# Routed experts on the tokens that chose them: a fused transformer block, before and after

## The reference, cut to what matters

```python
x = x + tanh(g_xattn[0]) * attention(layernorm(x), cache=ctx)           # stage A
x = x + tanh(g_ffn[0])   * ternary_ffn(layernorm(x))                    # hidden width 682
x = x + tanh(g_xattn[1]) * wkv(w, u, layernorm(x), ctx)                 # recurrence over 64 tokens
x = x + tanh(g_ffn[1])   * experts(layernorm(x))

def wkv_step(p, q, o, k, v):              # per channel, o is a running maximum
    no = maximum(o, u + k); A = exp(o - no); E = exp(u + k - no)
    y = (A * p + E * v) / (A * q + E)
    no2 = maximum(w + o, k); A2 = exp(w + o - no2); E2 = exp(k - no2)
    return (A2 * p + E2 * v, A2 * q + E2, no2), y

def experts(x):                           # 8 experts, F = 128, 2 of them for each token
    shared = silu(x @ shared_gate) * (x @ shared_up) @ shared_down      # FS = 256
    probs = softmax(x @ router_w); vals, ids = top_k(probs, 2)
    combine = zeros(N, 8).at[arange(N)[:, None], ids].add(vals)
    y = einsum("enf,efd->end", silu(x @ w_gate[e]) * (x @ w_up[e]), w_down)
    return shared + einsum("ne,end->nd", combine, y)
```

## Time and profile before

| what | value |
|---|---|
| median of 3 runs | 811.62 us (809.74 to 812.77) |
| span of the profiled execution, first to last instruction | 806.8 us |
| TensorE busy | 741.4 us, 92% |
| PE weight loads | 642.7 us, 80% |
| VectorE busy | 633.1 us, 78% |
| GpSimd busy | 398.0 us, 49% |
| ScalarE busy | 384.9 us, 48% |
| mean granted TensorE clock | 0.975 |

### The profile page before, as it was taken

The page is one execution under the profiler, slowest core; times in us unless marked ns, Lnnn a source line. Parts: engine busy times, 40 slices in busy tenths (PEclk is TensorE's granted clock), DMA queues, the critical chain, the costliest instruction groups (busy, mean ns, idle before and its releaser), DMA issues.

```text
span 806.8 us, 13118 instructions
## 1 busy us (share of the span) xinstructions
PE 741.4 (92%) x4582; PEld 642.7 (80%) x4582; DVE 633.1 (78%) x1043; ACT 384.9 (48%) x730; POOL 398.0 (49%) x382
## 2 busy tenths in 40 slices
PE   6988799889999999989998999989998999968896
PEld 5876687778888788878887888878887988746785
DVE  2857589687978798888989798888979797899532
ACT  3536434556355644654455645653465635431321
POOL 1024332364746365464636465455546464565364
PEclk8999979999999999999999999999999999988999
DMA  8170002010022013110032113110121000101121
GB/s 249 53 208 1 1 1 53 27 54 27 27 79 67 27 38 81 45 47 13 26 78 66 35 30 78 55 37 26 43 74 53 26 26 26 41 26 40 34 73 51
DMA packets 35895, 41.19 MB, mean 51 GB/s; under 512 B 3118, under 2 KB 27096, under 8 KB 35864
## 3 DMA queue, kind: packets, MB, share of 16 engines
q1 hardware_dynamic: 35864, 40.78, 17.6%
HBM read 36.45 MB, written 4.33 MB: 51 GB/s over the span
## 4 chain that ended last, share of the span: by engine, by line
PE 59%; DVE 15%; issue 4%; POOL 3%; ACT 1%; DMA 1%; DVEq 0%; POOLq 0%; ACTq 0%
PE sums L475 14%; PE gate_ps L475 13%; PE up_ps L475 12%; PE transit L475 6%; DVE wk L1389 3%; DVE wk L1394 3%; PE transit L540 3%; PE transit L467 3%; PE transit L552 3%; DVE wk L1396 2%; POOL act_sb L1139 2%; PE transit L520 1%; POOL hid_l L1130 1%; DVE act_sb L1379 1%; DVE za_l L1333 1%
## 5 line engine op out<-in xcount | busy, mean ns | idle before, releaser
L1130 POOL TENSOR_TENSOR hid_l<-act_sb,hid_h 128x512 fp32r<-128x512 f32 (+1 forms) x128 | 173.3, 1354 | 171.9 <-ACT hid_h L917 171.9
L917 ACT ACTIVATE hid_h<-act_sb 128x512 fp32r<-128x512 f32 (+1 forms) x128 | 80.4, 628 | 150.9 <-POOL act_sb L1139 117.8
L1139 POOL TENSOR_TENSOR act_sb<-act_sb,late 128x512 f32<-128x512 f32 x64 | 92.0, 1438 | 100.2 <-DVE act_sb L1381 80.9
L1379 DVE SCALAR_TENSOR_TENSOR act_sb<-act_sb,gate_ps 128x512 f32<-128x512 f32 (+1 forms) x128 | 85.8, 670 | 68.9 <-ACT act_sb L901 68.9
L475 PE MATMUL sums<-down_h,hid_h 128*128 128x256 f32 x320 | 92.3, 288 | 12.7 <-POOL hid_l L1130 12.7
L475 PE MATMUL sums<-down_h,hid_l 128*128 128x256 f32 x320 | 90.0, 281 | 0.0
L475 PE MATMUL sums<-down_l,hid_h 128*128 128x256 f32 x320 | 90.0, 281 | 0.0
L1381 DVE TENSOR_TENSOR act_sb<-act_sb,up_ps 128x512 f32<-128x512 f32 x120 | 82.4, 687 | 4.1
L901 ACT ACTIVATE act_sb<-gate_ps 128x512 f32<-128x512 f32 x80 | 47.2, 590 | 71.4 <-PE up_ps L475 66.1
L475 PEld LDWEIGHTS sums<-down_h,hid_h 128*128 128x128 f32 x320 | 60.9, 190 | 19.8 <-issue 17.9
L475 PE MATMUL gate_ps<-zm_h,gate_h 128*128 128x512 f32 x140 | 62.3, 445 | 5.6 <-DVE act_sb L1381 5.6
(11 more groups left out here) (194 smaller groups left out, 1962.7 us busy)
## 6 DMA issues: line engine op xcount, KB each, us to landing
late<-combine_rows SPq DMA_DIRECT2D x64, 256.0 KB, 3.2
ctx_tok<-in_ctx SPq DMA_DIRECT2D x8, 512.0 KB, 4.9
vals<-in_ctx SPq DMA_DIRECT2D x16, 256.0 KB, 5.6
out_x<-late SPq DMA_DIRECT2D x8, 512.0 KB, 3.2
xa<-in_x SPq DMA_DIRECT2D x7, 512.0 KB, 3.5
wk<-in_L_ffn_w SPq DMA_DIRECT2D x2, 682.0 KB
late<-in_L_ffn_w_down SPq DMA_DIRECT2D x1, 1024.0 KB, 6.6
wk<-in_L_ffn_w_gate SPq DMA_DIRECT2D x2, 512.0 KB, 4.4
```

What stands on the lines that cost most here:

```text
L917: nc.scalar.activation(hid_h[0:n, pos], act_sb[0:n, pos], ACT.Copy).then_inc(hid_h_set, 1)
L1130: nc.gpsimd.tensor_tensor(hid_l[0:n, pos], act_sb[0:n, pos], hid_h[0:n, pos].bitcast(F32), ALU.subtract).then_inc(hid_l_set, 1)
L1139: nc.gpsimd.tensor_tensor(act_sb[:, pos], act_sb[:, pos], comb_sb[:, pos], ALU.mult).then_inc(weighted, 1)
L1379: nc.vector.scalar_tensor_tensor(mine, mine, 1.0, gate_ps[pos][0:hidden_rows(chunk)], ALU.add, ALU.mult).then_inc(gated_one, 1)
```

## The change

It does six things.

- Stages get lags of their own: P (first normalisation of a block, z0), A (attention), F (its feed-forward), N (normalising F's result for the recurrence), W, M. All twelve turns, -1 to 10, are written out, with one order of the pieces on each engine; pieces of stages that are off in a turn fall away.
- M keeps the two shared chunks in the turn. The eight expert chunks leave it, and with them the combine weights' way through DRAM.
- In M's place in the turn, tokens get places in lists: the router gives each token a first and a second choice (rank 0 and 1); TensorE counts by matmuls with ones (`place`), VectorE makes place numbers (`dispatch`), and GpSimd scatters each token's row by indirect DMA into a list in DRAM, by expert and rank: 8 scatters for each block.
- After the loop SP ends the 16 lists with padding rows (`end_lists`), VectorE makes tables of which tile of 128 rows belongs to which expert, and 76 tiles (38 for each rank) run in 19 groups of four. SP reads a tile's row number into a register and loads the tile; TensorE transposes it, reads the expert's number into a register (twice for each tile) and runs 6 + 3 matmuls of 256 columns with that expert's weights; ScalarE, VectorE and GpSimd work on the group. Rank 0 results are scattered to rows in DRAM; for rank 1 GpSimd fetches those by indirect DMA, VectorE adds, and GpSimd scatters the sums to the output.
- F's chunks are pipelined one deep: up(c + 1), then down(c). On ScalarE tanh(c + 1) stands ahead of the high part of c.
- The recurrence goes without a running maximum: keys' exponentials come with the decay folded in by two more rows in the product z2_T, four scans run on them, and add_now is two fused operations.
- A turn's idle matmuls fall away but in the first turns.

The diff, cut; a line of "..." stands for what is left out. In order: the lists on top, SP, TensorE, ScalarE, GpSimd, VectorE.

```diff
-TRANSIT = [
-    ("A", "ctxT0"), ("A", "ctxT1"), ("M", "combT"), ("W", "z2T0"), ("W", "z2T1"), ("A", "z0T0"), ("A", "z0T1"),
-    ("A", "q0"), ("A", "q1"), ("A", "k0"), ("A", "k1"), ("A", "v0"), ("A", "v1"), ("A", "scores"), ("A", "pT"),
-    ("A", "oT0"), ("A", "oT1"), ("A", "wo0"), ("A", "wo1"), ("A", "z1T0"), ("A", "z1T1"), ("W", "yT0"), ("W", "yT1"),
-    ("W", "z3T0"), ("W", "z3T1"), ("W", "route"),
-LAG = {"A": 0, "W": 1, "M": 2}
+LAG = {"P": -1, "A": 0, "F": 1, "N": 1, "W": 2, "M": 3}
+TRANSIT = [
+    ("W", "z2T0"), ("W", "z2T1"), ("A", "q0"), ("A", "q1"), ("A", "k0"), ("A", "k1"), ("A", "ctxT0"), ("A", "ctxT1"),
+    ("A", "v0"), ("A", "v1"), ("A", "scores"), ("M", "place"), ("A", "pT"), ("A", "oT0"), ("A", "oT1"), ("A", "wo0"),
+    ("A", "wo1"), ("W", "yT0"), ("W", "yT1"), ("P", "z0T0"), ("P", "z0T1"), ("A", "z1T0"), ("A", "z1T1"),
+    ("W", "z3T0"), ("W", "z3T1"), ("W", "route"),
+CHUNKS = [("M", 0), ("M", 1)] + [("F", c) for c in range(6)]
+SUMS = [("M", "y"), ("F", "y")]
...
+RT = NTOK // P + E - 2
+CAP = NTOK + P
+PADS = E - 2
+ROWS = E * CAP + PADS * P
+NTILE = 2 * RT
+NG = NTILE // 4
...
+def end_lists(k, lst, cols):
+    for e in range(E):
+        end = sp.value_load(list_ends[0:1, k, e:e + 1], min_val=0, max_val=ROWS - P)
+        sp.dma_start(lst[bass.ds(end, P)], pad_rows[:, cols]).then_inc(ends_in, 16)
+def load_tile(j):
+    if j >= RING:
+        sp.wait_ge(y_out[(j - RING) % YRING], y_uses(j - RING))
+    k = rank(j)
+    lst, cols = (list0, list1)[k], COLS[k]
+    row = sp.value_load(tile_rows[0:1, k, j % RT:j % RT + 1], min_val=0, max_val=ROWS - P)
+    sp.dma_start(tiles[:, slot(j), cols], lst[bass.ds(row, P)]).then_inc(tiles_in[(j // 4) % 4], 16)
...
+def place(b):
+    pe.wait_ge(picks_set, b + 1)
+    bank, full = claim("M", "place", b)
+    to = bank[:, 0:2 * (NT + 1) * E].rearrange("p (k r e) -> p k r e", k=2, r=NT + 1)
+    all_ = ones[:].bitcast(F32R)
+    nc.tensor.matmul(to[:, :, 1:NT + 1], all_, picks[:], start=True, stop=False, skip_group_check=True)
+    nc.tensor.matmul(to[:, :, 0:NT], earlier[:], picks[:], start=False, stop=False, skip_group_check=True)
+    for back in range(2, NT + 1):
+        last = nc.tensor.matmul(to[:, :, back:NT + 1], all_, picks[:, :, 0:NT + 1 - back], start=False, stop=back == NT,
+                                skip_group_check=True)
+    last.then_inc(full, 1)
...
-    def f_up(c):
-        up(t, ("A", c))
-        if c >= 2:
-            down(t, ("A", c - 2))
...
-    m_up(9)
-    m_down(7)
-    if first:
-        keep_clock(6)
-    f_up(0)
-    m_down(8)
-    f_up(1)
-    if w:
-        y_T(t)
-    m_down(9)
-    f_up(2)
-    f_up(3)
-    f_up(4)
-    if w:
-        z_T(t, "W", "z3T", zw_row, 2)
-    f_up(5)
...
+    if w is not None:
+        z2_T(w)
+    if a is not None:
+        q_and_k(a)
+    if m is not None:
+        up(("M", 0), m)
+    if a is not None:
+        context_T(a)
+        values(a)
+    if m is not None:
+        up(("M", 1), m)
+        down(("M", 0), m)
+    if a is not None:
+        scores(a)
+    if a == 0:
+        abs_sums()
+        keep_clock(10)
+    if m is not None:
+        place(m)
+    f_up(0)
+    if m is not None:
+        down(("M", 1), m)
+    if a is not None:
+        probs_T(a)
+    f_up(1)
+    f_down(0)
+    if a is not None:
+        attend(a)
+    f_up(2)
+    f_down(1)
+    if a is not None:
+        project(a)
+    f_up(3)
+    f_down(2)
+    if w is not None:
+        y_T(w)
+    f_up(4)
+    f_down(3)
+    if p == 0:
+        keep_clock(12)
+    if p is not None:
+        z0_T(p)
+    f_up(5)
+    f_down(4)
+    if a == 0:
+        keep_clock(30)
+    if a is not None:
+        z1_T(a)
+    f_down(5)
+    if w is not None:
+        z3_T(w)
+        route(w)
...
+def experts_up(g, pair):
+    pe.wait_ge(zr_h_set, 2 * g + pair + 1)
+    wait_group_taken(pe, f"z{pair}", g)
+    if g >= 2:
+        pe.wait_ge(hidr_set, 2 * (g - 2) + pair + 1)
+    else:
+        pe.wait_ge(gated, ALL_CHUNKS)
+    for t in range(2):
+        j = 4 * g + 2 * pair + t
+        e = pe.value_load(tile_experts[0:1, rank(j), j % RT:j % RT + 1], min_val=0, max_val=E - 1)
+        o = gu_bank(g, pair)[:, t * D:(t + 1) * D]
+        for k in range(KH):
+            z_h, z_l = (z[:, g % 2, pair, t * D + k * P:t * D + (k + 1) * P] for z in (zr_h, zr_l))
+            w_h, w_l = (w_[:, k, SC:MC].rearrange("p e a f -> p e (a f)")[:, bass.ds(e, 1)].rearrange("p e n -> p (e n)")
+                        for w_ in (gu_h, gu_l))
+            last = split_product(o, (z_h, z_l), (w_h, w_l), k == 0, k == KH - 1)
+    last.then_inc(gu_full, 1)
...
+tiles_T(0)
+for g in range(NG + 1):
+    if g + 1 < NG:
+        tiles_T(g + 1)
+    if g < NG:
+        experts_up(g, 0)
+    if g > 0:
+        hidden_T(g - 1)
+    if g < NG:
+        experts_up(g, 1)
+    if g > 0:
+        experts_down(g - 1)
...
+    for h in range(KH):
+        bank = wait_full(act, "W", f"z2T{h}", b)
+        if b > 0:
+            act.wait_ge(yw_set, KH * (b - 1) + h + 1)
+        nc.scalar.activation(seqs(h, EK, 1), bank[:].rearrange("p (b s) -> p b s", b=NS), ACT.Exp).then_inc(free_of("W", f"z2T{h}", b), 1)
...
+    if w is not None:
+        key_weights(w)
+    if a is not None:
+        queries(a)
+        own_keys(a)
+    if m is not None:
+        squash(("M", 0), m)
+    if a is not None:
+        context_T(a)
+        values(a)
+    if m is not None:
+        squash(("M", 1), m)
+        high_hidden(("M", 0), m)
...
+    if a is not None:
+        softmax(a)
+    if m is not None:
+        high_hidden(("M", 1), m)
+    f_squash(0)
+    if a is not None:
+        probs_T(a)
+    f_squash(1)
+    f_high(0)
+    if a is not None:
+        attend(a)
...
+    f_squash(2)
+    f_high(1)
+    if a is not None:
+        keep_context(a)
...
+    f_squash(4)
+    f_high(3)
+    if p is not None:
+        high_z0(p)
+    f_squash(5)
+    f_high(4)
+    if a is not None:
+        normalise_attended(a)
+    f_high(5)
+    if a is not None:
+        high_z1(a)
+    if w is not None:
+        normalise_recurrent(w)
+    if n is not None:
+        normalise_fed(n)
+    if w is not None:
+        high_z3(w)
+        route(w)
...
+def scatter(b, r):
...
+    for k, (lst, cols) in enumerate(zip((list0, list1), COLS)):
+        nc.gpsimd.indirect_dma_start(
+            lst, bass.IndirectOffsetOnAxis(ap=place_no[:, k, r:r + 1], axis=0), row_out[:, r, cols], None,
+            bounds_check=ROWS - 1, oob_is_err=False).then_inc(scattered, 16)
...
+    f_low(0)
+    m_scatter(0)
+    f_low(1)
+    m_scatter(1)
+    if p is not None and p > 0:
+        row_factors("P", p)
+    f_low(2)
+    m_scatter(2)
+    if a is not None:
+        row_factors("A", a)
+    f_low(3)
+    m_scatter(3)
+    if w is not None:
+        row_factors("W", w)
+    f_low(4)
+    f_low(5)
+    if n is not None:
+        row_factors("N", n)
...
+for pair in range(PAIRS):
+    keep_halves(pair)
+for n in range(YRING):
+    pool.wait_ge(y_out[n], y_uses(max(j for j in range(RT) if j % YRING == n)))
+for pair in range(PAIRS, PAIRS + 3):
+    fetch_halves(pair)
+for pair in range(PAIRS, 2 * PAIRS):
+    give_out(pair)
+    if pair + 3 < 2 * PAIRS:
+        fetch_halves(pair + 3)
...
-def running_max(t, h):
-    wait_taken(dve, t, "W", f"z2T{h}")
...
-def exponents(t, h):
-    dve.wait_ge(omax_set, t.count("W", KH, h + 1))
-    nc.vector.scalar_tensor_tensor(seqs(h, A2, 1), seqs(h, OMAX, 0), decay_sb[:, h:h + 1], seqs(h, OMAX, 1),
-                                   ALU.add, ALU.subtract).then_inc(a2arg_set, 1)
-    nc.vector.scalar_tensor_tensor(flat(h, DELTA)[:, 0:TOK].rearrange("p (b s) -> p b s", b=NS), kw[:, h, :, 1:S1],
-                                   bonus_sb[:, h:h + 1], seqs(h, OMAX, 0), ALU.add, ALU.subtract).then_inc(delta_set, 1)
...
+def add_now(b, h):
+    dve.wait_ge(q_done, KH * b + h + 1)
+    nc.vector.scalar_tensor_tensor(seqs(h, EK, 1), seqs(h, EK, 1), gamma[:, h:h + 1], seqs(h, QS, 0), ALU.mult, ALU.add).then_inc(den_set, 1)
+    dve.wait_ge(p_done, KH * b + h + 1)
+    nc.vector.scalar_tensor_tensor(seqs(h, EV, 1), seqs(h, EV, 1), gamma[:, h:h + 1], seqs(h, PS, 0), ALU.mult, ALU.add).then_inc(num_set, 1)
...
+    if w is not None:
+        scans(w)
+    if m is not None:
+        gate(("M", 0), m)
+        gate(("M", 1), m)
+    if w is not None:
+        add_now(w, 0)
+    if a == 0:
+        channels()
+    if a is not None:
+        row_max(a)
+    if w is not None:
+        divide(w, 0, 0)
+        divide(w, 0, 1)
+    if m is not None:
+        dispatch(m)
+        add_shared(m)
...
+    if a is not None:
+        row_scale(a)
+    f_gate(0)
+    if w is not None:
+        quotient(w, 0)
+        add_now(w, 1)
+    f_gate(1)
+    if w is not None:
+        divide(w, 1, 0)
+        divide(w, 1, 1)
+        quotient(w, 1)
...
+    if p is not None and p > 0:
+        statistics_first(p)
+    if a is not None:
+        add_attention(a)
+        statistics_attended(a)
...
+    f_gate(3)
```

(16 more changed lines are left out.)

2070 lines of the change are left out of this document (970 added, 1100 removed).

## The result

Before 812.19 us, after **1132.47 us** (median of four, 1131.89 to 1137.62): a ratio of **1.395** [1.390, 1.400]. The kernel got slower, as forecast, and by almost twice the forecast amount: 320 us in place of 168.

The account below looks back on a forecast made before the run. TensorE was taken to bound six of ten turns. Loop 719, ahead of the list phase 48, list phase 199 and last rows 9 made 975; with 4.8 outside the span, 980 us, range 780 to 1100.

Parts of the forecast that it names:

- What goes: Work removed: TensorE's routed experts take 106 us in place of 267; VectorE in a steady turn falls from 76.0 to 53 to 55.
- The routed chunks were also the cover, and they leave the loop: In the loop: expert chunks gave TensorE work during other engines' hand-overs; without them, 30 us of holes in each turn.
- The walk of a full turn: Along TensorE's new order in the loop: a full turn of 81.5 us, 50.9 of matmuls and 30.6 of holes.
- I add 3 us a turn for that: Clock charge in a full turn: 5 us of matmuls at half speed, partly hidden, taking 81.5 to 84.5 us.
- the fourth rival: Half clock through the loop: eight blocks of 50.9 us of matmuls charged again, 1390 us in all; chance 0.02.
- The start: Loop's first turns: 57 us up to the first F matmul, then 69 without M and 62 without W too.
- The first rival: Waits in the loop are covered, each turn costs its busiest engine, VectorE's 55: 714 us in all; chance 0.20.
- The list phase: After the loop: 19.5 steps of mean 10.2 us, 199 in all, with 9 more for the last rows.
- with free reads 6.5 a step: List phase if register reads cost nothing: 6.5 us a step, set by VectorE's chain, 127 in all.
- its 7.5: List phase by the skill page's register load floor of about 0.6 us: 7.5 a step, 53 us less in all.
- Costed at nothing: Scatters in GpSimd's idle time, extra router operations, transfers of lists and padding to tiles were taken to add no time.
- The last recurrence: Loop's last recurrence turn: 46 us, the closing turn's 71, bound by VectorE, less about 25 of its work.

Follow-up runs that it names:

- experiment 8: The kernel before without its eight routed chunks, nothing put in their place, loop written out: 761.43 us, 0.938 of the kernel before.
- Experiments 1: The changed kernel with idle matmuls on TensorE in each hole of a turn, 22 of them ahead of the router: 1036.94 us, 1.272 of the kernel before.
- experiment 4: The changed kernel with idle matmuls in the holes, 34 in place of 22 ahead of the router: 1026.72 us, 1.263 of the kernel before.
- experiment 7: The changed kernel with 28 tile places for 16 and no TensorE register reads in the list phase: 1085.13 us, 1.335 of the kernel before.
- experiment 10: The changed kernel's work in other orders on four engines: first order 963.01 us, with 28 tile places 942.22, another order with 28 places 893.87.
- the second order: The changed kernel in another hand-written order, recurrence's rows turned after the projection, with 28 tile places: 893.87 us, 1.100 of the kernel before.
- experiment 9: The kernel before with the recurrence's VectorE work cut to 8 columns in all turns but the second: 781.51 us, 0.961 of the kernel before.

## Why the prediction was right in direction and wrong in size

**What goes** held: VectorE at 51.4, TensorE's records a third fewer. "The routed chunks were also the cover, and they leave the loop" is the whole case, and experiment 8 shows it without any of the change's other parts: take the chunks away, and the turn is as long as with them, in part by holes and in part by the clock.

**The walk of a full turn** held as a walk of waits. 30.6 us of holes were foreseen, 26.0 measured, each F hole 2.7 for 2.9. Experiments 1 and 4, less the clock loss that they keep, put the turn at 81 to 85 by estimate, near the 81.5 walked.

**The step that failed** is the one line behind it: "I add 3 us a turn for that". The clock cost 21 to 25 (102.4 less the walked 81.5; or 76.1 of busy time less the 50.9 of matmuls; the clock loss summed from the trace is 22.5). Of that, experiments 1 and 4 gave 13 to 17 back in a full turn. I charged the half clock once, behind the longest hole, since rows 7 showed one such stretch of 5 us. But the rows had no bound on how *often* it happens, and in the new turn it happens behind six of the seven holes ahead of a down, and in the turn's first 12 us, which run at 0.50 throughout. The closing turn's mean of 0.90, which I held against the fourth rival, was the mean of a turn with eight routed chunks in it, which the new turn hasn't got. In the six turns from the first full one to the one without attention the clock is most of the 101 us (72 + 21 + 8) by which they came out longer.

**The start** failed as well, a smaller term: "57, as now, nothing in it being much changed". That term ends where the next turn's work begins, since the 62 and 69 behind it are whole turns: at 68.1, 11 us of the 37 (8 of them idle matmuls on the chain, 58.3 to 66.1). The other 26 are the two turns, 157 in place of 131, with a granted clock of 0.75 between 80 and 221 and a clock loss of 28 us where the forecast has some 6.

**The fourth rival** was right in mechanism and half right in size. It charged every block's 50.9 us of matmuls twice; 21 to 25 were lost in a full turn. The Trainium skill's TensorE: Matmul & The Clock Gate (section Loop structure matters more than you think) has the matmuls of a loop run cold where each waits long for a DMA. The trace agrees behind the hole that ends at 474 (0.50 for 12 us), where the wait was a hand-over and not a DMA, though not for every burst (0.73 in the mean of a turn). A chance of 0.02 for it was far too small; as a graded term instead of all or nothing it would have been most of the truth.

**The first rival**, waits covered after all, is out: it wanted full turns below 65. The changed kernel's take 102, and the best other order tried has full turns of 68.8 to 71.9.

**The list phase** came out near (229 against 208) by luck: its terms were wrong in both directions. A read costs TensorE's queue 0.45, not 1.0; SP's read with its issue costs 1.17 (below), not 1.45; an indirect transfer 0.97 and 0.30 to issue the next, the 1.3 taken. The first half's 10 was a chain of reads in the forecast, and is a ring of places (10.4) with reads and slower clock right behind it (9.5); the second half's 10.4 was GpSimd's transfers, and these held (10.6 in experiment 7), with the ring making it 11.4 to 13.1 in most steps of the changed kernel; and there is a seam of 17.9 that I hadn't got. With the right reads my sum would have come out too low: VectorE's 6.5 in the first half and 10.4 in the second are 8.5 a step, 34 us less in all. By the same count the prediction's "with free reads 6.5 a step" and its 7.5 left out its own 10.4 for the second half. The Trainium skill's DMA: Bandwidth & Descriptors (section Latency and other measured facts) has about 0.6 us as a register load's floor. The trace is near it: 0.57 us from the last matmul's start ahead of a read to the next one's.

The rows on which that rests: SP's list ends in its queue's timeline (16 reads with their transfers), and GpSimd's indirect transfers in the page's groups.

```profile
873.64 18.77 SPq L493 DMA_DIRECT2D list<-wk  x16
```

```profile
L1235 POOL DMA_INDIRECT list<-row_out,place_no x64 | 64.8, 1012 | 29.0 <-issue 15.6 <-DVE row_out L1469 13.4
...
L1305 POOL DMA_INDIRECT half_out<-y_rows,tiles x38 | 37.0, 972 | 92.8 <-DVE y_rows L1715 86.7 <-issue 6.1
```

**Costed at nothing**: the scatters held. L1235's 64 stand in GpSimd's idle time, and no F hole is longer than the one in rows 4. The last recurrence (46) and the part ahead of the list phase (48 for 43.6) held too.

So the 320 us are, by parts of the span: the loop with its start, 858 where it had been 757, and the phase behind it, 273 in place of a last turn of 50. Of the first part the order is the cause: experiment 10 takes 220 us out of the loop with the same work. Of the second part ring and reads are 47 us (experiment 7); the rest is the serial phase itself, which no run took apart further.

What stays open: why the second order still leaves the turn's clock at 0.88. Its slow stretches are the turn's beginning (from 390.6, among the router's matmuls, to 397), 404 to 408 with TensorE busy throughout, and the end and the wake of its hole of 6.2 us (442 to 448). Whether a list phase with steps of 6 us behind a loop in the second order would beat 777 us was not tried.

## What to carry to other kernels

Work that fills the waits of others can be worth almost nothing to remove: before taking matmuls away from a pipelined loop, walk what TensorE will wait for when they are gone, or cut them out for one run and look. Charge the clock at every hole and not at the longest alone, because a hole of under 3 us can double the price of the burst behind it. And of a change in several parts try each alone: here a recurrence worth 34 us lay inside a rewrite that cost 320.

## What the runs showed of the hardware that was not expected

- The granted clock fell to 0.50 with TensorE busy throughout, among transposes and products two rows deep that came behind matmuls of 8 and 16 columns (experiment 4, at 383.2).
- One hole of under 3 us was followed by 12 us of unbroken matmuls at half clock (474 to 486; 32 of the 48 are attend's, of 64 columns).
- Some VectorE operations took as long as the GpSimd operation beside them. In the timeline of all engines, experiment 9 first and then the kernel before:

```profile
339.67 1.36 DVE L1396 SCALAR_TENSOR_TENSOR wk<-kw,bonus_sb,wk 128x8 f32<-128x8 f32 x1
339.67 2.57 POOL L1112 TENSOR_TENSOR wk<-kw,wk 128x512 f32<-128x512 f32 x2
...
347.82 1.78 DVE L1396 SCALAR_TENSOR_TENSOR wk<-kw,bonus_sb,wk 128x512 f32<-128x512 f32 x1
...
351.21 0.74 DVE L1396 SCALAR_TENSOR_TENSOR wk<-kw,bonus_sb,wk 128x512 f32<-128x512 f32 x1
```

Eight columns took 1.36 us beside a GpSimd operation of 1.3. The same operation on all 512 columns took 1.78 beside one of 1.76 (L1112 at 347.30), and 0.74 where GpSimd ran nothing (350.74 to 353.35). It reads two tensors from SBUF; L1379, which takes one of its two from PSUM, took 0.69 beside GpSimd (347.39 in experiment 9). So the 1.75 us of L1394 look like waiting for GpSimd more than work; no run tried it.
